# A planner's rule for letting a unit wait when VectorE's coming rounds are full

## What is computed

```python
# 1: a causal depthwise convolution (4 taps) and a linear state recurrence
u = conv(xn @ W_in + b_in)                       # 512 channels
h = einsum('ij,bdj->bdi', tanh(A), h) + u_t[..., None] * Bp    # over 512 steps
y = einsum('j,bdj->bd', Cp, h) + Dp[0] * u_t
out1 = silu(y) @ W_out + b_out
# 2: attention, 16 heads of 16 channels, no mask
q, k, v = split(xn @ W_qkv + b_qkv)
out2 = softmax(q @ k.T / 4) @ v
# 3: 8 experts of 256 x 256, the two largest gates of each token
gate = softmax(xn @ W_gate + b_gate); combine = top-2 of gate
out3 = sum_e combine[e] * (xn @ W_experts[e] + b_experts[e])
```

## Time and profile before

| | |
|---|---|
| median of 3 runs | 788.93 us (787.6 to 789.32) |
| profiled execution | 787.89 us, of which the span between first and last instruction is 786.1 us |
| TensorE busy | 753.9 us, 96% of the span |
| VectorE busy | 581.4 us, 74% |
| ScalarE busy | 535.4 us, 68% |
| GpSimd busy | 387.4 us, 49% |
| mean granted TensorE clock | 0.994 of full speed |

### The profile page before, as it was taken

The page is one execution under the profiler, slowest core; times in us unless marked ns, Lnnn a source line. Parts: engine busy times, 40 slices in busy tenths (PEclk is TensorE's granted clock), DMA queues, the critical chain, the costliest instruction groups (busy, mean ns, idle before and its releaser), DMA issues.

```text
span 786.1 us, 13228 instructions
## 1 busy us (share of the span) xinstructions
PE 753.9 (96%) x4404; PEld 453.3 (58%) x4404; DVE 581.4 (74%) x846; ACT 535.4 (68%) x926; POOL 387.4 (49%) x522
## 2 busy tenths in 40 slices
PE   9689999999998999999999999989999999999996
PEld 7457556565555655556555665556655565555553
DVE  6689876976679875887759876698667987568920
ACT  4637766777666767667567775667666776767775
POOL 8445554455444834456346463445444473435654
PEclk9989999999999999999999999999999999999999
DMA  8301201122110221102111121113111121112000
GB/s 272 69 4 44 68 19 28 38 59 78 35 38 13 79 58 41 42 22 82 35 42 42 45 82 31 38 25 95 42 42 43 32 58 39 46 41 69 23 2 27
DMA packets 32465, 39.09 MB, mean 50 GB/s; under 512 B 8513, under 2 KB 18535, under 8 KB 32398
## 3 DMA queue, kind: packets, MB, share of 16 engines
q1 hardware_dynamic: 31418, 37.29, 18.1%
q10 hardware_dynamic: 980, 0.96, 0.6%
HBM read 8.74 MB, written 4.19 MB: 16 GB/s over the span
## 4 chain that ended last, share of the span: by engine, by line
PE 80%; DVE 13%; issue 4%; ACT 3%; ACTq 0%; DVEq 0%
PE PS L464 39%; PE PS L624 12%; PE SB L591 12%; PE TB L608 7%; PE PS L521 5%; DVE mx L1051 4%; PE PS L480 2%; DVE ys L901 2%; DVE xn L1027 1%; PE PS L631 1%; DVE xl L933 1%; DVE qkl L927 1%; DVE ys L897 1%; PE PS L476 1%; DVE th L1086 1%
## 5 line engine op out<-in xcount | busy, mean ns | idle before, releaser
L1051 DVE TENSOR_REDUCE mx<-SB 128x2 f32<-128x1024 f32 x256 | 312.9, 1222 | 141.0 <-PE SB L591 139.9
L1118 POOL TENSOR_TENSOR acc<-acc,mt 128x256 f32<-128x256 f32 x320 | 247.9, 782 | 251.0 <-ACT mt L675 178.9
L830 ACT ACTIVATE Pt<-TB 128x1024 f32<-128x1024 f32 x251 | 257.7, 1027 | 59.3 <-PE TB L608 56.3
L675 ACT ACTIVATE mt<-PS,cpad 128x256 f32<-128x256 f32 x256 | 107.5, 471 | 58.9 <-PE PS L464 58.5
L591 PE MATMUL SB<-kst,qst 48*128 48x512 f32 x512 | 127.9, 496 | 14.6 <-DVE mx L1051 14.3
L624 PE MATMUL PS<-Pt,V 128*17 128x512 f32 x1024 | 122.3, 595 | 0.0
L591 PEld LDWEIGHTS SB<-kst,qst 48*128 48x128 f32 x512 | 47.7, 183 | 125.3 <-DVE mx L1051 75.1
L464 PE MATMUL PS<-weh,xTh 128*128 128x512 f32 x256 | 109.9, 429 | 2.2 <-DVE xTl L914 1.3
L608 PE MATMUL TB<-qst,kst 50*128 50x512 f32 x502 | 101.2, 398 | 1.1 <-ACT Pt L830 1.0
L464 PE MATMUL PS<-wel,xTh 128*128 128x512 f32 x256 | 100.9, 394 | 0.0
L464 PE MATMUL PS<-weh,xTl 128*128 128x512 f32 x256 | 100.6, 393 | 0.0
(11 more groups left out here) (162 smaller groups left out, 1142.6 us busy)
## 6 DMA issues: line engine op xcount, KB each, us to landing
qst<-qkh SPq DMA_DIRECT2D x124, 64.0 KB, 2.3
kst<-qkh SPq DMA_DIRECT2D x124, 64.0 KB, 2.3
out<-acc SPq DMA_DIRECT2D x8, 512.0 KB, 2.8
qst<-qkl SPq DMA_DIRECT2D x62, 64.0 KB, 2.2
kst<-qkl SPq DMA_DIRECT2D x62, 64.0 KB, 2.3
acc<-in_x SPq DMA_DIRECT2D x7, 512.0 KB, 3.9
Bt<-in_wexp SPq DMA_DIRECT2D x2, 512.0 KB, 7.6
raw<-in_wexp SPq DMA_DIRECT2D x2, 512.0 KB, 8.8
```

The source lines that it names most:

```text
L675: return e.activation(mt[:, item % NM, :], P, ACT.Copy, scale=scale)
L830: e.activation(Pt[:, T % NP, :, :], turned_bank(T)[:, :, :], ACT.Exp, scale=0.25).then_inc(s_ex, 1)
L1051: e.tensor_reduce(mx[:, g % 2, 0:2, 4 * jj + a], SB[:, :, :], AX.X, ALU.max).then_inc(s_mx, 1)
L1118: e.tensor_tensor(v, v, mt[:, item % NM, :], ALU.add).then_inc(s_mt, 1)
```

## The change

A table `PATIENCE` and a test `crowded` are added. A unit T, Q, Z or Y is passed over in round t if that round lies before its patience ends (32 times its batch plus the table's value) and if one of the rounds that its VectorE work falls in would be loaded with more than 3.0 us. V, C, M and O are never passed over (V has VectorE costs, but its patience has always ended). The planner then takes the next unit of the list that may be done. The rule for Z in front of a values product stays. Nothing else is changed.

```diff
+PATIENCE = {("T", 0): -16, ("T", 1): -16, ("Z", 0): 2, ("Q", 0): -8, ("Q", 1): -8, ("Q", 2): 8, ("Q", 3): 8}
+PATIENCE.update({("Y", i): 4 * i + 8 for i in range(4)})
...
+    def crowded(kind, b, i, t):
+
+        if kind == "Z" and values_at(t + 1):
+            return True
+        late = kind == "Z"
+        return (t < 32 * b + PATIENCE.get((kind, i), -99)
+                and any(vector[t + late + k] + us > 3.0 for k, us in VECTOR[kind].items()))
...
-            k = next((k for k, u in enumerate(todo) if soonest(*u) <= t and not (u[0] == "Z" and values_at(t + 1))), None)
+            k = next((k for k, u in enumerate(todo) if soonest(*u) <= t and not crowded(*u, t)), None)
```

## The result

The changed kernel took **795.66 us** (median of 4 runs, 794.38 to 795.92) beside 789.12 us (787.6 to 789.38) of the kernel before on the same chip: a ratio of 1.0082 with a 95% interval of 1.007 to 1.0095. It is slower by 0.8%, where 11.8 us less was forecast. The profiled execution took 795.92 us with a span of 794.1, where the kernel before had 787.89 and 786.1: 8.0 more.

What follows compares the result with a forecast made beforehand. TensorE was taken to bound the kernel, with 17.6 us of excess in rounds 32 to 254 where VectorE takes over. Gains 7.6 + 3.6 + 0.6 + 0 = 11.8 us gave 776.5 us, range 772 to 780 (chance 0.72).

Steps and rivals of the forecast that it cites:

- point 2: Overfull rounds in 32 to 254: excess falls from 11.6 to 4.0 us as those left stand apart; 7.6 gained.
- point 5: Start, rounds 7 to 31: two Q units move from 7 to 8; 0 us net, bounds -1.5 to +1.5.
- point 1: TensorE's unit work unchanged, 0 us; round 7 becomes empty, its four added idle matmuls fit in VectorE's time.
- point 6: Queues: nothing added; a late T pair, as in round 113, put at 0.2 us in each of six batches.
- Rival A: Only the Z rounds and half of the rest gain: 7 us faster, 781 to 782 us; chance 0.15.
- Point 3: Z's second-half rounds: excess in rounds 32 to 254 falls from 5.4 to 1.8 us, 3.6 gained.
- Point 4: Round 226: an M unit takes the place of the lone C unit, 0.6 us gained.
- Rival C: VectorE's convs slowed by GpSimd's additions: 19 us lost against 11.8 gained, 795 us; chance 0.07.
- Rival B: Nothing moves: losses could sit in ScalarE's same-round hand-offs, so the excess stays, 786 to 790 us; chance 0.06.

Runs made afterwards that it cites:

- joined rows: Rows written out by hand: rounds 0 to 31 of the kernel before, 32 to 255 of the changed kernel; 788.25 us, ratio 0.9994.
- The two places filled: Joined rows with T0 one round earlier, then units moved only in rounds 121 to 125 and 172 to 178; 783.04 us, ratio 0.9924.
- place 1: Rounds 121 to 125 in the two places filled: O3.1 joins M3.13, M3.15 joins M3.14; whole run 783.04 us.
- two reductions: The kernel before with two unused VectorE reductions added in each of six quiet rounds; 791.5 us, ratio 1.0036.
- the run with three reductions: The kernel before with three unused VectorE reductions added in each of six quiet rounds; 798.33 us, ratio 1.0117.

## Why the prediction was wrong, point by point

**The balance.** The forecast for the profiled execution was 776.1 us, and it took 795.9, 19.8 more. 11.7 us of this stand in point 2, where 4.0 us were to stay and 15.7 did, and 8.0 in point 5. Z gave 0.4 more than forecast, and 0.35 lie ahead of round 7.

**Point 5, the start, is the step that turned the sign.** "0, bounds -1.5 to +1.5" measured 8.0 us in the trace and 7.4 in time (joined rows). Three of its terms were mis-sized or missing. The catching up of round 7 was put at 1.4 us and was 3.0: point 1 says that the idle matmuls "fit in what VectorE needs for the round anyway", which they do (they end before its maximum starts), but so had the 2.8 us of the two Q units, which then had to be done in the open. The 2.27 us gap ahead of the scores of round 8 was followed by half a clock, which the step doesn't have at all; with the clock kept up, rounds 7 and 8 lose 1.8 us less. And the split of `wout` was put at 0.6 us in round 14, priced from a round in which GpSimd added less. Beside more M units it took 4.1 instead of 2.7 us, and rounds 13 to 16 lost 3.6 us (the spread split gave 3.5 us back). The 1.4 us more of rounds 9 to 12 were not tried by themselves.

The Trainium skill (TensorE: Matmul & The Clock Gate, "HAM oscillation — how this bites in real kernels") describes a kernel in which TensorE's wait between groups of matmuls lets the clock drop, and the next group starts at half rate. The rows of this case agree at 55.44 us, where the clock fell during the wait. At 83.34 and 351.54 us the next group started at full rate, and the clock fell 1.6 and 1.0 us later. The waits of the skill's example are for a DMA and are put at about 3 to 5 us; all three here are shorter. Its example would still have suggested a rival in the prediction: the price of a wait is the wait and the slow matmuls behind it.

**Point 2, the overfull rounds,** was right about the places it looked at: 10.3 became 1.2 us, 9.1 gained for 7.6. What failed is "4.0 stay" for all of the rest. The measure counted VectorE work above 3.0 us, the limit of the rule itself, while most rounds hold 2.24 to 2.51 us of TensorE's work. Rounds 122 to 124, planned at 2.95, 2.95 and 2.35, pass the rule and take 3.15, 2.91 and 2.96 us for 2.24, 2.51 and 2.24: they lose 0.9, 0.4 and 0.7, and none can give back to the next. The two places filled bear this out in part (1.1 of the 2.5 us of place 1). Nor do the overfull rounds stand apart after the change: by the planner's own costs, 78 and 79, 86 and 87, 145 and 146, 206 and 207, 214 and 215, and 217 and 218 follow one another above 3.0. (Its costs, worked through again, give 44 rounds with 40.2 us over the line before and 29 with 21.5 after, not 38.1 and 26 with 20.4; the proportion, and so the 6.2, is the same.) "A lone overfull round costs nothing" holds for as much as the next round gives back, 0.7 to 0.8 us; beyond it six lone overloads cost 0.4 us each with two reductions and 1.6 with three.

**The T pairs** (point 6, 0.2 us each) measured 1.2, 1.1 and 3.2 us in rounds 49, 113 and 177, and in round 73 0.6, which the next rounds gave back. Moving T0 alone took back 0.9 us in 113 and none in 177. There a row with 1.7 us of TensorE's work stood behind M units whose additions held `yl`, and with it the tanh and the exponential. With an M unit in that row and T6 out of it, 2.5 of the 3.2 us are gone, and with them the fall of the clock, which had given up 1.7. Rival A had named this with "rounds 113 and 114 lose a microsecond", and its sign was still wrong.

**Point 3, Z,** was right: lone second halves lose nothing (round 129), those beside P 0.5 each where 0.6 was said, 4.0 gained for 3.6. **Point 4:** 0.6 gained. **Point 1:** the units are the same, but eight matmuls more ran.

**Rival C** gave 795 us, nearly the time measured, but by another way, so that this is chance. The convs' mean rose from 919 to 956 ns, far from 1.1 us:

```profile
L912 DVE SCALAR_TENSOR_TENSOR ys<-uc,cwc,ys 128x511 f32<-128x511 f32 (+2 forms) x96 | 91.7, 956 | 0.0
```

In kind it was at work at one place, the split of `wout`. **Rival B** ("the losses sit in the hand-offs", 0.06) was the nearest for rounds 32 to 254: the excess stayed, 17.3 for 17.6. Its cause is borne out in part. The prediction set it aside because VectorE waited for `xh` only 10.3 us in all; that wait fell to 8.6, but the one for a T unit's `xTh` went from nothing to 7.9 us, and with T0 a round earlier it shrank together with the loss of round 113.

What stays open: the changed rule gives other rows in 166 rounds, and of the 9.0 us in "all other rounds" only rounds 121 to 124 were tried by themselves. Whether a limit that follows TensorE's work of each round would do better than 3.0 was not tried.

## What to carry to other kernels

When a planner balances two engines, compare the second engine's load with the first engine's load in the same slot, not with a fixed limit (shown here at one place, not for a whole plan), and let it see every hand-off (the bank, the other queues), or relieved slots are paid for in others. Before emptying a slot, ask what ran there unseen beneath the other engine's work: it will have to be done in the open. A wait of TensorE near two microseconds may cost a half-clock stretch on top of itself (1.8 us where it was taken away). And test an order with rows written out by hand: a switch in a greedy planner moves everything behind it, and measures that too.

## What was not expected of the hardware

The granted clock fell to 0.50 with single waits of TensorE of 1.79, 2.27 and 2.71 us: in the second during the wait, in the others 1.0 and 1.6 us after matmuls had begun again. Whether it falls is not told by the length of the last wait alone. With 1.65 us it stayed at 1.00 in the kernel before and fell in the run with three reductions (0.50 from 527.5 to 530.9 us), in the same round of the same rows:

```profile
519.33 0.50 PE L591 MATMUL SB<-kst,qst 48*128 48x512 f32 x2 [1.65 <-DVE mx L1051]
```

```profile
525.63 0.50 PE L594 MATMUL SB<-kst,qst 48*128 48x512 f32 x2 [1.65 <-DVE mx L1054]
```

Also, all kernels of this study have the same rows up to round 6, and of their seventeen profiled executions five have a fall at about 49.5 to 53 us, in these rows, and twelve have none. A fall between 46 us and the last matmuls lasted 3.4 or 6.8 us and gave up 1.7 or 3.4 us. And VectorE's piece of the split of `wout` (a `scalar_tensor_tensor` with two inputs from SBUF) took 0.41 us without GpSimd beside it and 0.95 beside GpSimd's additions: slower by 0.54 us, less than the 0.74 us or more that one such addition lasts.
